# A state-space scan followed by neighbourhood attention: scan units of 64 channels and two states, with three additions handed to TensorE

## The chip, the cores and the metric

One Trainium2 chip, one of its cores. The metric is the device time of one execution in microseconds; the time before is the median of three runs. Engines are called TensorE (PE in the rows), VectorE (DVE), ScalarE (ACT), GpSimd (POOL) and SyncE (SP, which here only issues DMAs).

## The reference

Input x has 4 images of 96 channels and 1024 positions. The first layer is a bidirectional state-space model; the second, neighbourhood attention, is not touched by the change. Cut to the first:

```python
x_norm = layernorm(x_flat) * gamma + beta
x_in = jnp.concatenate([x_norm, x_norm[:, ::-1]], axis=0)      # 8 sequences of 1024 steps
xr, z = jnp.split(x_in @ W_in, 2, axis=-1)                     # 192 channels each
xr = silu(causal_depthwise_conv4(xr) + conv_b)
dbl = xr @ W_xproj                                             # 6 + 16 + 16 columns
dt = softplus(dbl[..., :6] @ W_dt + b_dt); Bm, Cm = dbl[..., 6:22], dbl[..., 22:]
def step(h, inp):                                              # 192 channels x 16 states
    h = exp(dt_t[:, :, None] * A) * h + (dt_t * x_t)[:, :, None] * B_t[:, None, :]
    return h, einsum('ben,bn->be', h, C_t)
y = (ys + xr * D) * silu(z)
out = (out_fwd + out_rev) * 0.5 + x_flat                       # out = y @ W_out
```

## The kernel before

**Tiles and units.** The 8 sequences of 192 channels are cut into 12 tiles of 128 rows (`TILE_ORDER`): an "L" tile holds channels 0 to 127 of one sequence, an "H" tile the channels 128 to 191 of two images. A tile has 16 units, one for each state, so there are 192 units k. For each unit:

- TensorE copies row n of B over all channels: two bf16 products with the 0/1 matrix `pick` (`spread_b`, L369) put it into one of two PSUM slots `bu`. The product for unit k+1 may start only when the scan of unit k-1 has freed its slot. B is held in `st` as three bf16 pieces that add up to the f32 value.
- ScalarE computes a = exp(dt * A) (`decay`, L564), two units ahead.
- VectorE multiplies `bu` by u = dt * x (`times_b`, L724) and scans along the positions (`scan`, L734).
- GpSimd multiplies the states by C (`read_out`, L690). C comes back from DRAM spread over the rows, in `c_rep`, by a DMA on SyncE's queue.
- TensorE adds the product to `y_ps` with an identity matrix (`sum_states`, L390), three units later (`SUM_LAG`).

**Work between units.** All else is a list of jobs written out by hand, `PLAN`: (unit at which TensorE starts it, name, arguments). Each job fills one of the two halves of `f_ps`, and ScalarE (VectorE for "out") empties it; a job waits until the job two before it has been emptied (`free`). In unit k TensorE issues, in this order, the B products of unit k+1, the jobs of unit k (`front`), and the sum of unit k-3. "conv" is the convolution as four taps, one tap a unit; "xp" the projection to B, C and the low-rank dt; "dt" the product before the softplus; "z" the gate; "cen" and "var" the layernorm; "out" the output product. ScalarE empties a job in the unit after its last one, behind that unit's `decay`.

**Softplus and the pieces of B.** ScalarE makes four pieces of the softplus (L505 to L519); GpSimd adds three of them (L639, L643, L647) and multiplies by x (L652). Of B, ScalarE rounds to bf16, GpSimd subtracts (L628), ScalarE rounds again (L494, L495), GpSimd subtracts again (L634). GpSimd also adds the two directions' x for the skip term D * x (L659), which VectorE adds to `y_ps` (L712) before it multiplies by the gate (L716).

**Before the first unit** the engines run the same jobs for the first tile in an order of their own (the lists in front of `for k in range(UNITS)`).

Of the kernel before, what the change touches and what calls it, by code (L numbers as in the profile page):

```python
# [9 lines left out]
ALU = mybir.AluOpType  # L10
# [11 lines left out]
A_RING, H_RING, HC_RING, C_RING, SUM_LAG = 3, 3, 4, 4, 3  # L22
ROWS = 3 * 2 * N_ST + RANK
LOADS = [4, 7, 12, 8]
# [27 lines left out]
def cols(th, n=HALF):  # L52
# [7 lines left out]
XR_SLOT = (0, 1, 2, 3, 4, 5, 3, 6, 0, 4, 1, 5)  # L60
XR_TILES = 7
STEPS = {"conv": TAPS, "xp": 2}

FIRST = [("cen", 0), ("var", 0), ("cen", 1), ("var", 1), ("conv", 0), ("conv", 2), ("xp", 0, 0), ("dt", 0),
         ("conv", 1)]

PLAN = [
# [4 lines left out]
    (49, "var", 2, 0), (50, "var", 2, 1), (51, "dt", 4, 0), (52, "dt", 4, 1), (53, "cen", 3, 0), (54, "cen", 3, 1),  # L72
    (56, "var", 3, 0), (57, "var", 3, 1), (58, "conv", 6, 0), (62, "conv", 6, 1), (66, "dt", 5, 0), (67, "dt", 5, 1),
    (68, "conv", 7, 0), (72, "conv", 7, 1), (76, "z", 1, 0), (77, "z", 1, 1), (78, "out", 0, 0, 0),
    (79, "out", 0, 0, 1), (79, "xp", 2, 0, 0), (81, "xp", 2, 0, 1), (84, "dt", 6, 0), (85, "dt", 6, 1),
    (86, "z", 2, 0), (87, "z", 2, 1), (88, "conv", 8, 0), (92, "conv", 8, 1), (97, "xp", 3, 0, 0), (99, "xp", 3, 0, 1),
    (101, "dt", 7, 0), (102, "dt", 7, 1), (103, "out", 1, 1, 0), (104, "out", 1, 1, 1), (105, "out", 2, 0, 0),
    (106, "out", 2, 0, 1), (107, "out", 2, 1, 0), (108, "out", 2, 1, 1), (109, "conv", 9, 0), (113, "dt", 8, 0),
    (114, "dt", 8, 1), (115, "conv", 9, 1), (119, "conv", 10, 0), (123, "conv", 10, 1), (128, "xp", 2, 1, 0),
# [3 lines left out]
    (168, "out", 3, 2, 0), (169, "out", 3, 2, 1), (182, "z", 5, 0), (183, "z", 5, 1), (184, "out", 4, 2, 0),  # L83
    (185, "out", 4, 2, 1), (186, "out", 4, 3, 0), (187, "out", 4, 3, 1)]
LAST = [("out", 5, 3, 0), ("out", 5, 3, 1)]
JOBS = [f + (th,) for f in FIRST for th in range(2)] + [p[1:] for p in PLAN] + LAST
# [3 lines left out]
SKIP_AT = (42, 60, 75, 142, 158, 171)  # L90
# [26 lines left out]

def mamba(nc, t, x1, bn_stats, c_d):

    with ExitStack() as ctx:  # L120
# [20 lines left out]
        pick = sb("pick", [ROWS - RANK, N_ST, 128], BF16)  # L141
# [8 lines left out]
        dt = sb("dt", [128, 2, L])  # L150
        u = sb("u", [128, 2, L])
        z = sb("z", [128, L])
        y = sb("y", [128, 3, L])
        dbc = sb("dbc", [ROWS, 4, L])
# [23 lines left out]
        st_rest = sem("st_rest")  # L178
        st_mid = sem("st_mid")
        st_done = sem("st_done")  # L180
        soft_act = sem("soft_act")
        soft = sem("soft")
        z_ready = sem("z_ready")
        skip_sum = sem("skip_sum")
        y_copied = sem("y_copied")
        y_skip = sem("y_skip")
# [14 lines left out]
        def bank(*job):  # L201
            return f_ps[:, J(*job) % 2, :]
# [13 lines left out]
        def _(sp):  # L216
            def both(column, name):
# [11 lines left out]
                 (pick_f, t["pick"]), (ident[:, :], t["ident"]), (a_neg[:, 0, :], t["A_log"][0:E_LO]),  # L229
                 (a_neg[0:E_HI, 1, :], t["A_log"][E_LO:E_IN]), (a_neg[E_HI:128, 1, :], t["A_log"][E_LO:E_IN])] +  # L230
# [6 lines left out]
            for group, done in zip(groups, loaded):  # L237
                for dst, src in group:
                    sp.dma_start(dst, src).then_inc(done, 16)
            for k in range(UNITS):  # L240
                tile, n = divmod(k, N_ST)
                if n == 0:
                    for b, d in tile_seqs(tile):
                        sp.wait_ge(c_stored[seq_slot(b, d)], 16 * (b // 2 + 1))
                if k >= C_RING:
                    sp.wait_ge(hc_done, k - C_RING + 1)
                kind, i, d = TILE_ORDER[tile]
                if kind == "L":
                    sp.dma_start(c_rep[:, k % C_RING, :], c_d[2 * i + d, n:n + 1, :].to_broadcast([128, L]))\
                        .then_inc(c_in[k % C_RING], 16)  # L250
                else:
                    for part in range(2):
                        sp.dma_start(c_rep[E_HI * part:E_HI * part + E_HI, k % C_RING, :],
                                     c_d[2 * (2 * i + part) + d, n:n + 1, :].to_broadcast([E_HI, L]))\
                            .then_inc(c_in[k % C_RING], 16)

        def c_loads(k):

            return sum(len(tile_seqs(i // N_ST)) for i in range(k % C_RING, k + 1, C_RING))
# [1096 lines left out]
```

## Time and profile before

| | |
|---|---|
| median of 3 runs | 1227.54 us (1224.55 to 1229.1) |
| the profiled execution, its own time | 1225.61 us |
| its span, first to last instruction | 1223.7 us |
| before the first unit | 0 to 55.0 us |
| the 192 units | 55.0 to 771.5 us |
| second layer | from about 782 us |
| busy in the stretch 55 to 772 us | VectorE 677.4, TensorE 642.6, GpSimd 595.6, ScalarE 440.3 of 717 us |
| granted TensorE clock there | 0.95 of 2.4 GHz on average |

The busy times add up, engine by engine, what ran; they don't tell what was waited for. That is read from the idle time just before an instruction and from what ended it. A wait of an engine that has slack costs nothing.

### The profile page before, as it was taken

To read this page: it belongs to the slowest core of one execution; us is meant where nothing else is said; L and a number is where in the kernel's file an instruction comes from. 1 tells how busy PE (TensorE), PEld (TensorE's weight loads), DVE (VectorE), ACT (ScalarE), POOL (GpSimd) and SP (SyncE) were. 2 spreads that over 40 slices of the span, in tenths; PEclk is the share of its full clock that TensorE was granted. 3 is DMA by queue.
4 is the path that set the end of the run, shared out by engine and by line. 5 is a ranking of instruction groups with operands and counts; after the bars stand their busy time and mean duration, and the time that the engine had idled before them with its cause. 6 is when DMAs were issued, how large, how long until landed. Compare 5 with 4: busy or idle time off the path is not lost. (4 is left out here: it accounts for less than half of the span.)

```text
span 1223.7 us, 9473 instructions
## 1 busy us (share of the span) xinstructions
PE 1078.3 (88%) x3294; PEld 369.1 (30%) x3294; DVE 964.5 (79%) x635; ACT 549.0 (45%) x574; POOL 878.0 (72%) x348
## 2 busy tenths in 40 slices
PE   7789999889988999989978878599999999996675
PEld 2233333333232333324322222223333333332221
DVE  1499999899998999999989999600296796969771
ACT  5755857796657464756573634111111020110321
POOL 0079799888878778978988966400098969789890
PEclk9879999899999989998988989879999999998787
DMA  2144355434354434453434444163849595682502
GB/s 78 71 141 151 140 157 137 156 123 153 121 157 123 153 122 138 136 173 126 170 121 138 133 144 136 25 153 76 129 102 188 84 204 83 141 133 39 107 1 73
DMA packets 106863, 150.95 MB, mean 123 GB/s; under 512 B 62818, under 2 KB 75848, under 8 KB 106816
## 3 DMA queue, kind: packets, MB, share of 16 engines
q1 hardware_dynamic: 104832, 143.65, 44.7%
q10 hardware_dynamic: 1984, 6.70, 2.0%
q8 instruction: 26, 0.43, 0.1%
q14 instruction: 21, 0.17, 0.1%
HBM read 123.27 MB, written 10.70 MB: 109 GB/s over the span
## 5 line engine op out<-in xcount | busy, mean ns | idle before, releaser
L690 POOL TENSOR_TENSOR hc<-h,c_rep 128x1024 f32<-128x1024 f32 x192 | 451.2, 2358 | 175.7 <-DVE h L734 169.5
L734 DVE TENSOR_TENSOR_SCAN h<-a,bu 128x1024 f32<-128x1024 f32 x192 | 439.0, 2286 | 20.1 <-ACT a L564 2.4
L390 PE MATMUL y_ps<-hc,ident 128*128 128x512 f32 x768 | 384.7, 625 | 2.9 <-POOL hc L690 1.7
L564 ACT ACTIVATE a<-dt,a_neg 128x1024 f32<-128x1024 f32 x192 | 218.6, 1148 | 224.5 <-DVE h L734 216.6
L724 DVE TENSOR_TENSOR bu<-bu,u 128x1024 f32<-128x1024 f32 x192 | 232.1, 1209 | 16.2 <-PE bu L369 16.2
L1147 POOL TENSOR_TENSOR prod_p<-vw,at 128x3584 f32<-128x3584 f32 x18 | 130.2, 7235 | 124.2 <-DMA vw<-v_d 120.8
L390 PEld LDWEIGHTS y_ps<-hc,ident 128*128 128x128 f32 x768 | 145.3, 197 | 213.3 <-issue 188.7
L1028 PE MATMUL sc_ps<-x,w_up 128*64 128x512 f32 x672 | 177.6, 604 | 0.0
L1028 PE MATMUL sc_ps<-x,w_low 96*64 96x512 f32 x672 | 177.3, 603 | 0.0
L369 PE MATMUL bu<-st,pick 96*64 96x512 bf16 (+1 forms) x512 | 120.2, 394 | 47.0 <-DVE h L734 41.3
L1098 ACT ACTIVATE sc<-sc_ps,rel 128x512 f32<-128x512 f32 x24 | 16.6, 690 | 248.4 <-PE sc_ps L1028 248.4
L1154 POOL TENSOR_TENSOR prod_p<-prod_p 128x1536 f32<-128x1536 f32 (+1 forms) x36 | 104.6, 2904 | 2.8
L1230 DVE TENSOR_REDUCE e_ps<-at 128x32 f32<-128x1568 f32 x6 | 17.6, 2932 | 106.4 <-DMA at<-scores_d 106.4
L369 PEld LDWEIGHTS bu<-st,pick 96*64 96x64 bf16 (+1 forms) x512 | 29.1, 104 | 194.7 <-DVE h L734 136.0
L1147 DVE TENSOR_TENSOR prod_v<-vw,e_ps 128x3584 f32<-128x3584 f32 (+1 forms) x24 | 86.8, 3616 | 0.5
L1250 DVE TENSOR_TENSOR acc_ps<-acc_ps,prod_v 128x1024 f32<-128x1024 f32 x66 | 81.3, 1232 | 2.3
L1028 PEld LDWEIGHTS sc_ps<-x,w_up 128*64 128x64 f32 x672 | 49.1, 137 | 100.6 <-issue 100.6
L1028 PEld LDWEIGHTS sc_ps<-x,w_low 96*64 96x64 f32 x672 | 49.3, 136 | 99.1 <-issue 99.1
L287 PE MATMUL f_ps<-xn,w_taps 96*128 96x512 f32 x128 | 68.6, 637 | 5.8 <-ACT t L507 2.9
L1044 PE MATMUL g_ps<-x,c_w 96*128 96x512 f32 x48 | 31.3, 811 | 26.6 <-DVE x L1222 26.6
L1120 ACT ACTIVATE up<-g_ps,c_b 128x512 f32<-128x512 f32 x24 | 16.5, 689 | 70.9 <-PE g_ps L1044 70.9
L564 ACT ACT_TABLE_LOAD x27 | 34.6, 1283 | 0.5
(124 smaller groups left out, 928.3 us busy)
## 6 DMA issues: line engine op xcount, KB each, us to landing
c_rep<-c_d SPq DMA_DIRECT2D x128, 512.0 KB, 3.6
c_rep<-c_d SPq DMA_DIRECT2D x128, 256.0 KB, 3.9
vw<-v_d SPq DMA_DIRECT2D x24, 532.0 KB, 9.6
x<-qk SPq DMA_DIRECT2D x66, 171.0 KB, 6.4
scores_d<-sc ACTq DMA_DIRECT2D x24, 196.0 KB
at<-scores_d SPq DMA_DIRECT2D x24, 196.0 KB, 4.7
x<-qk SPq DMA_DIRECT2D x22, 152.0 KB, 6.7
v_d<-v SPq DMA_DIRECT2D x4, 541.5 KB, 6.2
```

Of the source, the lines that this page charges most:

```text
L287: mm = pe.matmul(out, w_taps[:, j, 0:E_LO], xn[:, i, s:s + HALF], start=(j == 0), stop=(j == TAPS - 1))
L369: mm = pe.matmul(bu[rows, k % 2, cols(th)], pick[:, n, 0:rows.stop - rows.start], st[:, seq_slot(b, d), cols(th)], start=True, stop=True)
L390: mm = pe.matmul(y_ps[:, cols(th)], ident[:, :], hc[:, k % HC_RING, cols(th)], start=(n == 0 and d == 0), stop=(n == N_ST - 1))
L564: nc.scalar.activation(a[:, k % A_RING, :], dt[:, tile % 2, :], ACT.Exp, scale=a_neg[:, kind_of(tile), n:n + 1]).then_inc(exp_done, 1)
L690: nc.gpsimd.tensor_tensor(hc[:, k % HC_RING, :], h[:, k % H_RING, :], c_rep[:, k % C_RING, :], ALU.mult).then_inc(hc_done, 1)
L724: nc.vector.tensor_tensor(bu[:, k % 2, :], bu[:, k % 2, :], u[:, tile % 2, :], ALU.mult)\
L734: nc.vector.tensor_tensor_scan(scan_order(h[:, k % H_RING, :], d), scan_order(a[:, k % A_RING, :], d), scan_order(bu[:, k % 2, :], d), 0.0 ...
L1028: mm = pe.matmul(sc_ps[64 * i:64 * i + 64, th, :], w[:, dx, :], x4[0:rows, (2 * p + i) % X4_RING, y:y + 16, dx:dx + W], start=(dx == 0 and ...
L1044: pe.matmul(bank(n)[:, :], c1_w[:, 128 * m:128 * m + 128], x1[:, b, cols(th)], start=True, stop=True).then_inc(job_done, 1)
L1147: return engine.tensor_tensor(prod, shifted, e[:, lo:hi].unsqueeze(2).broadcast_to([128, hi - lo, HD, W]), ALU.mult)
L1154: nc.gpsimd.tensor_tensor(prod_p[:, lo[0]:lo[1]], prod_p[:, lo[0]:lo[1]], prod_p[:, hi[0]:hi[1]], ALU.add).then_inc(pp, 1)
L1250: nc.vector.tensor_tensor(acc_v, acc_v, prod_v[:, k:k + 2], ALU.add).then_inc(pv, 1)
```

## The change

A unit now holds 64 channels in two states: rows 0 to 63 the even state, rows 64 to 127 the odd one. Two units, one for each half of a tile's channels, follow each other, and `sum_states` adds both, with a 128x64 matrix `fold` that adds the two states as well. dt and u must therefore lie twice, once in each half of the rows: SyncE's queue copies them by halves. On TensorE there are three new kinds of jobs: "sum" adds the four pieces of the softplus, "rest" and "low" make the differences of B, and the skip term is a product with a diagonal matrix. Each is taken off GpSimd or VectorE. ScalarE empties both halves of `f_ps` in one instruction. A job that took several units, one tap or part in each, now does its first half in one unit and its second half in the next ("conv", "sum"), or both halves in one unit ("xp", "rest", "low", "dt").

```diff
-A_RING, H_RING, HC_RING, C_RING, SUM_LAG = 3, 3, 4, 4, 3
+A_RING, H_RING, HC_RING, C_RING, SUM_LAG = 3, 3, 4, 4, 4
-STEPS = {"conv": TAPS, "xp": 2}
+STEPS = {"conv": 2, "sum": 2}
...
-    (0, "xp", 1, 0, 0), (2, "xp", 1, 0, 1), (5, "dt", 1, 0), (6, "dt", 1, 1), (7, "conv", 3, 0), (11, "conv", 3, 1),
...
+    (0, "xp", 1, 0), (2, "rest", 1, 0), (3, "dt", 1), (5, "low", 1, 0), (7, "sum", 1), (9, "conv", 3), (12, "conv", 5),
+    (14, "dt", 2), (18, "sum", 2), (21, "xp", 0, 1), (23, "rest", 0, 1), (24, "conv", 4), (26, "low", 0, 1),
...
             for k in range(UNITS):
...
+                for part in range(2):
+                    sp.dma_start(c_rep[E_HI * part:E_HI * part + E_HI, k % C_RING, :],
+                                 c_d[2 * b + d, 2 * m + part:2 * m + part + 1, :].to_broadcast([E_HI, L]))\
                         .then_inc(c_in[k % C_RING], 16)
...
+                for t_next in range(1, N_TILES):
+                    since = k - AT[("sum", t_next)]
+                    if since == 6:
+                        left(sp, J("sum", t_next, 1))
+                        second_half(dt, t_next, dt_b)
+                    if since == 8:
+                        sp.wait_ge(u_done, t_next + 1)
+                        sp.wait_ge(dt_b, 32 * (t_next + 1))
+                        first_half(dt, t_next, dt_a)
+                        second_half(u, t_next, u_b)
+                    if since == 9:
+                        sp.wait_ge(u_b, 32 * (t_next + 1))
+                        first_half(u, t_next, u_a)
...
+            def rest_job(b, d, th):
+
+                rows = slice(0, ROWS - RANK)
+                out = bank("rest", b, d, th)[rows, :]
+                free(J("rest", b, d, th))
+                pe.wait_ge(st_high, SEQS.index((b, d)) + 1)
+                pe.matmul(out, ident[rows, rows], dbc[rows, b % 2, cols(th)], start=True, stop=False)
+                pe.matmul(out, minus_i[rows, rows], st[rows, seq_slot(b, d), cols(th)], start=False,
+                          stop=True).then_inc(job_done, 1)
...
+            def sum_job(tile, th):
+                n = J("sum", tile, th)
+                free(n)
+                pe.wait_ge(soft_act, 4 * tile + 4)
+                for i, part in enumerate((t3, t4, dt[:, tile % 2, 1, :], dt[:, tile % 2, 0, :])):
+                    mm = pe.matmul(bank("sum", tile, th), ident[:, :], part[:, cols(th)], start=(i == 0), stop=(i == 3))
                 mm.then_inc(job_done, 1)
...
                 for th in range(2):
-                    mm = pe.matmul(y_ps[:, cols(th)], ident[:, :], hc[:, k % HC_RING, cols(th)],
-                                   start=(n == 0 and d == 0), stop=(n == N_ST - 1))
-                mm.then_inc(summed, 1)
+                    for half in range(2):
+                        rows = slice(E_HI * half, E_HI * half + E_HI)
+                        mm = pe.matmul(y_ps[rows, cols(th)], fold[:, :], hc[:, (k + half) % HC_RING, cols(th)],
+                                       start=False, stop=(m == N_ST // 2 - 1))
+                mm.then_inc(summed, 2)
...
             for k in range(UNITS):
                 spread_b(k + 1)
+                if k >= SUM_LAG and k % 2 == 0:
+                    sum_states(k - SUM_LAG)
                 front(k)
-                if k >= SUM_LAG:
-                    sum_states(k - SUM_LAG)
...
             softplus(0)
-            middle(0, 0)
+            rest_left(0, 0)
+            low_left(0, 0)
             for th in range(2):
                 conv_left(1, th)
...
                 dve.wait_ge(summed, N_ST * (r + 1))
-                dve.wait_ge(skip_sum, g + 1)
-                nc.vector.scalar_tensor_tensor(out=y_ps[:, :], in0=xr_of(f), scalar=d_skip[:, kind:kind + 1],
-                                               in1=y_ps[:, :], op0=ALU.mult, op1=ALU.add).then_inc(y_skip, 1)
```

**TensorE before the first unit.** Before, from the end of "xp" (L307) and the dt product of the first tile (L317) over the conv of tile 1 (L287) to the B products of the first two units (L369):

```order
L307 MATMUL f_ps<-xr,w_x 102x512
L317 MATMUL f_ps<-dbc,w_dt 128x512 x2
L287 MATMUL f_ps<-xn,w_taps 128x512 x8
L369 MATMUL bu<-st,pick 128x512 x4
L303 MATMUL f_ps<-xr,w_x 102x512
```

Of the change, from the dt product to the same conv (dt L374, conv L326; L352 to L364 are "rest" and "low"):

```order
L374 MATMUL f_ps<-dbc,w_dt 128x512 x2
L352 MATMUL f_ps<-dbc,ident 96x512
L353 MATMUL f_ps<-st,minus_i 96x512
L352 MATMUL f_ps<-dbc,ident 96x512
L353 MATMUL f_ps<-st,minus_i 96x512
L362 MATMUL f_ps<-dbc,ident 32x512
L363 MATMUL f_ps<-st,minus_i 32x512
L364 MATMUL f_ps<-mid,minus_i 32x512
L362 MATMUL f_ps<-dbc,ident 32x512
L363 MATMUL f_ps<-st,minus_i 32x512
L364 MATMUL f_ps<-mid,minus_i 32x512
L326 MATMUL f_ps<-xn,w_taps 128x512 x8
```

"rest" and "low" now stand ahead of the conv of tile 1.

**TensorE around units 50 to 53,** where tile 3 begins. Before, units 50 and 51: "var" (L275) and "dt" (L317), `y` put back into `y_ps` (L387), the sums (L390) and the B products (L369):

```order
L369 MATMUL bu<-st,pick 128x512 x2
L275 MATMUL f_ps<-var,center 96x512
L390 MATMUL y_ps<-hc,ident 128x512 x2
L369 MATMUL bu<-st,pick 128x512 x2
L317 MATMUL f_ps<-dbc,w_dt 128x512
L387 MATMUL y_ps<-y,ident 128x512 x2
L390 MATMUL y_ps<-hc,ident 128x512 x2
```

Of the change, from the sums in unit 50 to the B products behind those of unit 52 ("sum" L383, `y` put back L459, skip term L461, sums L467, B products L440):

```order
L467 MATMUL y_ps<-hc,fold 64x512 x4
L383 MATMUL f_ps<-t,ident 128x512 x2
L383 MATMUL f_ps<-dt,ident 128x512 x2
L440 MATMUL bu<-st,pick 128x512 x2
L383 MATMUL f_ps<-t,ident 128x512 x2
L383 MATMUL f_ps<-dt,ident 128x512 x2
L440 MATMUL bu<-st,pick 128x512 x2
L459 MATMUL y_ps<-y,ident 128x512 x2
L461 MATMUL y_ps<-xr,diag_d 128x512 x2
L467 MATMUL y_ps<-hc,fold 64x512 x4
L440 MATMUL bu<-st,pick 128x512 x4
```

Four f32 products of "sum" now stand between two sets of B products, where there was one product of "var" or "dt" with two of the sums.

## Rows read from the trace of the kernel before

**Rows 1.** Page, part 1: busy us, share of the span, instructions.
```profile
PE 1078.3 (88%) x3294; PEld 369.1 (30%) x3294; DVE 964.5 (79%) x635; ACT 549.0 (45%) x574; POOL 878.0 (72%) x348
```
**Rows 2.** Timeline of one unit at 307 us: start, us, engine, line.
```profile
307.44 1.21 DVE L724 TENSOR_TENSOR bu<-bu,u 128x1024 f32<-128x1024 f32 x1
307.58 0.60 PE L369 MATMUL bu<-st,pick 96*128 96x512 bf16 x2
...
308.12 1.08 PE L291 MATMUL f_ps<-xn,w_taps 96*64 96x512 f32 x4
...
308.74 2.29 DVE L734 TENSOR_TENSOR_SCAN h<-a,bu 128x1024 f32<-128x1024 f32 x1
...
309.13 1.98 PE L390 MATMUL y_ps<-hc,ident 128*128 128x512 f32 x4
...
310.94 1.21 DVE L724 TENSOR_TENSOR bu<-bu,u 128x1024 f32<-128x1024 f32 x1
...
311.08 0.60 PE L369 MATMUL bu<-st,pick 96*128 96x512 bf16 x2
```
**Rows 3.** Waits of VectorE, 55 to 772 us: total us, times, longest.
```profile
DVE bu L724 <- PE bu L369: 16.2, 9, 3.9
DVE h L734 <- ACT a L564: 2.4, 3, 1.6
DVE x L702 <- PE f_ps L337: 2.2, 1, 2.2
DVE y_ps L712 <- PE y_ps L390: 1.9, 2, 1.7
DVE h L734 <- issue: 0.9, 2, 0.5
```
**Rows 4.** Groups by line: busy us, mean ns, idle before.
```profile
L712 DVE SCALAR_TENSOR_TENSOR y_ps<-xr,d_skip,y_ps 128x1024 f32<-128x1024 f32 x6 | 7.7, 1285 | 3.1 <-PE y_ps L390 2.9
...
L690 POOL TENSOR_TENSOR hc<-h,c_rep 128x1024 f32<-128x1024 f32 x192 | 451.2, 2358 | 175.7 <-DVE h L734 169.5 <-PE y_ps L390 6.2
```
**Rows 5.** Timeline of TensorE, 20 to 34 us, two convs.
```profile
19.69 7.11 PE L287 MATMUL f_ps<-xn,w_taps 96*128 96x512 f32 x16 [0.59 <-ACT var L432]
26.73 7.09 PE L291 MATMUL f_ps<-xn,w_taps 96*64 96x512 f32 x32
```
**Rows 6.** Timeline, a late B product, 224 to 232 us.
```profile
224.61 1.06 ACT L494 ACTIVATE st<-dbc 32x1024 bf16<-32x1024 f32 x1 [5.37 <-POOL dbc L628]
...
227.27 2.02 PE L271 MATMUL f_ps<-x,center 96*96 96x512 f32 x2 [5.04 <-ACT z L432]
...
231.75 0.60 PE L369 MATMUL bu<-st,pick 96*128 96x512 bf16 x2
...
232.38 1.23 DVE L724 TENSOR_TENSOR bu<-bu,u 128x1024 f32<-128x1024 f32 x1 [3.89 <-PE bu L369]
```
**Rows 7.** Timeline, TensorE at the full clock, 235 to 238 us.
```profile
235.19 1.88 PE L390 MATMUL y_ps<-hc,ident 128*128 128x512 f32 x4
...
236.91 0.60 PE L369 MATMUL bu<-st,pick 96*128 96x512 bf16 x2
...
237.35 1.02 PE L275 MATMUL f_ps<-var,center 96*96 96x512 f32 x2
```
**Rows 8.** Timeline before the first unit, 42 to 57 us.
```profile
42.19 8.83 PE L287 MATMUL f_ps<-xn,w_taps 96*128 96x512 f32 x16 [0.59 <-ACT t L507]
...
46.44 1.15 ACT L519 ACTIVATE u<-u,minus_one 128x1024 f32<-128x1024 f32 x1
...
47.62 1.05 ACT L494 ACTIVATE st<-dbc 32x1024 bf16<-32x1024 f32 x1
...
51.06 0.69 ACT L432 ACTIVATE xr<-f_ps,conv_b 128x512 f32<-128x512 f32 x1 [0.73 <-PE f_ps L287]
...
54.13 1.28 ACT L609 ACT_TABLE_LOAD   x1
...
56.61 2.29 DVE L734 TENSOR_TENSOR_SCAN h<-a,bu 128x1024 f32<-128x1024 f32 x1 [0.33 <-ACT a L564]
```
**Rows 9.** Windows: stretch, its us, busy of PE, PEld, DVE, ACT, POOL, then PEclk.
```profile
640.00:650.00 10.00, 6.69 (x22) 2.31 (x21) 9.73 (x7) 3.46 (x3) 10.00 (x5) 1.00 0.35 105
...
720.00:730.00 10.00, 7.06 (x11) 2.79 (x12) 9.79 (x7) 2.30 (x2) 4.71 (x2) 0.66 0.33 107
```
**Rows 10.** Timeline of ScalarE at a softplus, 378 to 386 us, and TensorE behind it.
```profile
378.41 1.04 ACT L512 ACTIVATE t<-t 128x1024 f32<-128x1024 f32 x1
...
382.80 1.15 ACT L519 ACTIVATE u<-u,minus_one 128x1024 f32<-128x1024 f32 x1
...
384.49 2.02 PE L287 MATMUL f_ps<-xn,w_taps 96*128 96x512 f32 x2 [2.29 <-ACT z L432]
```
**Rows 11.** DMA issues: KB each, median us to landing.
```profile
c_rep<-c_d SPq DMA_DIRECT2D x128, 256.0 KB, 3.9
```

More of the change, by code:

```diff
@@ L85 @@
-LAST = [("out", 5, 3, 0), ("out", 5, 3, 1)]
-JOBS = [f + (th,) for f in FIRST for th in range(2)] + [p[1:] for p in PLAN] + LAST
+    (0, "xp", 1, 0), (2, "rest", 1, 0), (3, "dt", 1), (5, "low", 1, 0), (7, "sum", 1), (9, "conv", 3), (12, "conv", 5),
+    (14, "dt", 2), (18, "sum", 2), (21, "xp", 0, 1), (23, "rest", 0, 1), (24, "conv", 4), (26, "low", 0, 1),
+    (28, "z", 0), (30, "dt", 3), (32, "cen", 2), (34, "sum", 3), (36, "var", 2), (38, "xp", 1, 1), (40, "rest", 1, 1),
+    (42, "low", 1, 1), (44, "cen", 3), (46, "dt", 4), (48, "var", 3), (50, "sum", 4), (54, "conv", 6),
@@ L87 @@
+    (125, "rest", 3, 1), (126, "dt", 9), (128, "low", 3, 1), (130, "sum", 9), (142, "dt", 10), (146, "sum", 10),
+    (158, "dt", 11), (162, "sum", 11), (168, "z", 4), (169, "out", 3, 2), (184, "z", 5), (186, "out", 4, 2),
+    (187, "out", 4, 3)]
+LAST = [("out", 5, 3)]
+JOBS = [j + (th,) for j in FIRST + [p[1:] for p in PLAN] + LAST for th in range(2)]
+AT = {p[1:]: p[0] for p in PLAN}
 DONE_AT = {p[1:]: p[0] + STEPS.get(p[1], 1) for p in PLAN}
@@ L240, in _, with first_half @@
+            def first_half(pairs, tile, done):
+                sp.dma_start(pairs[high, tile % 2, 0, :], pairs[low, tile % 2, 0, :]).then_inc(done, 16)
+            sp.wait_ge(soft_first, 3)
+            first_halves(dt, dt_a, dt_b, dt[:, 1, 0, :])
+            sp.wait_ge(u_done, 1)
+            first_halves(u, u_a, u_b, u[:, 1, 0, :])
             for k in range(UNITS):
[L241 to L244, printed above, removed]
+                tile, m, half, (b, d) = unit(k)
+                if k % N_ST == 0:
+                    for seq in tile_seqs(tile):
+                        sp.wait_ge(c_stored[seq_slot(*seq)], 16 * (seq[0] // 2 + 1))
@@ L257, in c_loads @@
         def c_loads(k):
-            return sum(len(tile_seqs(i // N_ST)) for i in range(k % C_RING, k + 1, C_RING))
+            return 2 * (k // C_RING + 1)
         @block.tensor
@@ new lines, in low_job @@
+            def low_job(b, d, th):
+                rows = slice(0, 2 * N_ST)
+                out = bank("low", b, d, th)[rows, :]
+                free(J("low", b, d, th))
+                left(pe, J("rest", b, d, 1))
+                pe.matmul(out, ident[rows, rows], dbc[rows, b % 2, cols(th)], start=True, stop=False)
+                pe.matmul(out, minus_i[rows, rows], st[rows, seq_slot(b, d), cols(th)], start=False, stop=False)
+                pe.matmul(out, minus_i[rows, rows], mid[rows, cols(th)], start=False,
+                          stop=True).then_inc(job_done, 1)
@@ L741, in front @@
                     if name == "out" and at == k:
[L742 to L743 removed]
+                        for th in range(2):
+                            add_out(*job, th)
+                tile, n = divmod(k - SUM_LAG + 2, N_ST)
                 if n == 0 and 0 < tile <= N_TILES and TILE_ORDER[tile - 1][2] == 1:
@@ L780, in _ @@
             for _, *job in LAST:
-                add_out(*job)
+                for th in range(2):
+                    add_out(*job, th)
             left(dve, len(JOBS))
```

453 lines of the change are left out of this document (225 added, 228 removed), and 6 rows, old and new, of the table PLAN.

## The prediction

> **What bounds the kernel now.** The page's busy times [rows 1] give TensorE the largest share of the span, but the two layers have different limits, so I read the stretches first: the change touches only the first layer, and its 192 units take 716.5 of 1223.7 us. The timeline of one unit [rows 2] shows who sets the pace there. VectorE multiplies (1.21 us), scans (2.29 us), and multiplies again 3.50 us after the first time, with no idle time between. TensorE's B product for a unit starts when the scan has freed its slot, then comes a job, then the sum, which ends at about the time when the next B product may start. VectorE is full, and TensorE nearly. 192 x 3.50 is 672 us; the rest is gates, output additions and waits. The waits of VectorE [rows 3] add up to 23.6 us, 16.2 of them for a B product. What makes one late stands in [rows 6]: ScalarE waited 5.37 us for a subtraction on GpSimd, so it emptied a bank late, TensorE waited 5.04 us for that bank, and the next B product, in line behind it, was 3.89 us late for VectorE. So of everything on the other engines only what delays a B product counts, and VectorE's own work.
>
> **What the change takes from VectorE.** The six skip additions of 1.285 us [rows 4], one of them at the very end: -7.7 us. Multiplications and scans stay 192 of each, with the same shape; a unit of 64 channels and two states is as long as one of 128 channels. GpSimd loses some five operations of about 2.4 us a tile. It was no bound (it waited 169.5 us for the scan, [rows 4]), so this gives nothing by itself, but the waits of ScalarE on it, as in [rows 6], go. I take all 23.6 us of old waits away and count the new ones afresh.
>
> **TensorE, unit by unit.** Costs at the full clock. Two f32 products of 512 columns, 1.72 us from start to start, so 0.86 each; the two B products, 0.44, taken as 0.45 [rows 7]. Products 64 columns wide, two at a time on the two halves of the array, cost 7.09 us for 8 pairs in a conv, against 7.11 us for 8 whole products [rows 5]: a pair costs as much as one. The four products with `fold` thus take 1.72 us for two units, where two units took 3.44 before. I add 0.15 for the turn from 128 to 64 columns: in [rows 2] one such pair took 1.01 us from 308.12 to the next start at 309.13, not 0.86. (TensorEngine Tiling (Array Packing) of the Trainium skill, section Key Properties, says that changing the tiling mode drains the engine; that speaks against this change, which turns twice in each two units, and the 1.01 us agrees with it.)
>
> A unit without a job thus costs TensorE 0.45 us when odd and 2.32 when even. But the new list puts half a "conv" or half a "sum", four f32 products or 3.44 us, into one unit: 3.89 us odd, 5.76 even. The start of a backward tile costs 5.76 too, without a job (0.45, 1.72 to put `y` back, 1.72 skip term, 1.87 sums). The average falls: over all units my costs sum to about 545 us, and TensorE was busy 642.6 of 717 us before. What counts is the lump. There are two slots for B: the product of unit k+1 can't start before scan k-1 ends and must be there 3.50 us later, and from its start to VectorE's go [rows 6] 0.63 us pass (231.75 to 232.38). So TensorE may be 2.87 us late and no more. I carry the lateness along (late + cost - 3.50, not below zero) and book what is over 2.87 as a wait of VectorE.
>
> - Units 50 to 52, "sum" then a backward tile's start: 2.26, 2.65, 4.91, a wait of 2.0 us. The same stands at 36, 68, 148 and 164 (at 36 with "var" in place of the put-back): five times, 10.3 us.
> - Unit 84, half a "sum" with a tile's start: 9.20 us, a wait of 4.3. Unit 116, "sum", start and "rest": 2.6.
> - Units 7 to 14, "sum", two convs, "dt": 2.8. Units 18 to 26, "sum", start, "xp", conv, "low": 3.0. Units 58 and 120, convs: 1.3 and 1.4. Units 100 and 132: 0.7 together.
>
> That is 26.4 us. By the same sums the old list, with one tap a unit, comes to no wait at all: a unit there costs 0.45 + 1.72 + 0.86, about 3.0 of 3.50 us.
>
> **ScalarE.** A softplus holds it from the first exponential to the end of the fourth piece for 5.5 us (378.41 to 383.95, [rows 10]), behind a `decay` of 1.15 and before a table load of 1.28: 8 us in a unit of 3.50. "sum" stands two units (7.0 us) behind the softplus's unit and needs all four pieces, which are ready after 6.7 us if ScalarE began on time. Where it has emptied a conv, "low" or "var" just before, it hasn't: at six tiles I find TensorE waiting for about 1 us, at unit 7 2.7, and at unit 82 ("rest" behind "xp" and softplus) 3.2. Such a wait was seen before: 2.29 us, [rows 10]. Part of it falls on lumps already late. I add 10 us (bounds 0 and, if every one of them came straight on VectorE, 14, with more where the clock is low, below).
>
> **Before the first unit.** Before, softplus ended at 47.6 us and the conv of tile 1 had begun on TensorE at 42.19 [rows 8]; ScalarE emptied its second half at 51.06, and VectorE scanned 5.5 us later, at 56.6. Now "rest" and "low" stand ahead of this conv. ScalarE now waits for both halves of "xp" and of "dt" and empties them in one go, about 0.45 us later each time, and is at 48.5 with the softplus; then two pieces of B, 1.05 us each as in [rows 8]: 50.6. "low" on TensorE, four f32 products and four bf16 ones, about 2.7: 53.3. ScalarE empties it: 54.4. The conv's first half waits for that bank, and its 8 products take 7.1 [rows 5] to 8.8 us [rows 8]: 61.5 to 63.2. From there two more table loads, the SiLU and `decay`: 5.5 us, so the first scan at 67 to 69, 10.4 to 12.1 us later than before. The row nearest in time is the 8.8, so I take +12. The copies of dt and u don't set this: u is ready at about 53.5, and four such transfers, at 3.9 us to landing for one [rows 11], are there by about 60.
>
> **SyncE's copies later.** A tile's copies are issued 6 to 9 units after "sum", and "sum" is at least 13 units ahead of its tile, except tile 1, with 9. There the last one leaves about 2.5 units ahead (C for unit k goes out when unit k-4 is read), waits for one landing, and lands again after 3.9 us; 1 to 2 us are to spare. I count nothing; without that margin it would cost up to 4 us, once.
>
> **The clock.** Full-clock costs are a lower bound. In 720 to 730 us TensorE was busy 7.06 of 10 us at a granted clock of 0.66, in 640 to 650 us with 6.69 at 1.00 [rows 9]: at that load it falls at times. Two units without a job now keep TensorE busy for 2.8 of 7.0 us, less than either row. Between jobs late in the list (units 133 to 141, 149 to 157, 170 to 183) the clock may be at 1.2 GHz when "dt", "sum" or a tile's start comes. I take 6 us for this, between 0 and 25, what the same sums give with every TensorE cost 10% up.
>
> **The sum.** -23.6 -7.7 +26.4 +10 +6 +12 = +23 us. Against the profiled execution's 1225.6 us: 1248.7. That execution was 1.9 us below the median, so **1250 us**.
>
> **Rivals.** *The lumps are hidden* (0.14, faster): TensorE's load per unit falls by a sixth, and if a lump of two units' length reached VectorE nowhere, only -23.6 -7.7 +12 stayed: 1208 us. It decides at lateness 2.87 us; against it stands that a B product 3.9 us late cost VectorE just that [rows 6]. *They cancel* (0.10): waits of 10 to 25 us where I count 42, with a shorter setup: 1222 to 1234, no change. *The clock falls* (0.12): half the clock in the sparse stretches makes half a "sum" 6.9 us long; some 10 jobs at 2 us or more: about 1270. TensorE: Matmul & The Clock Gate of the Trainium skill, Part 1, states that the throttled clock is the default and activity lifts it; by that rule this rival is likelier than I have it, and rows 9 bear it out only half. *The pairs don't overlap* (0.04): 96 x 1.72 us more, TensorE at 710 us over VectorE's 672: above 1300; [rows 5] speak against it. *Copies come late or C behind them* (0.04): some 4 us a tile, about 1290. What is left, 0.56, is the forecast, 1235 to 1262.
>
> Measurement tells about 0.5%, 6 us, from no change. Faster: the first rival and the lower tail, 0.16. Same 0.10. Slower 0.74. The range reaches from the upper part of the first rival, 1214, to the clock rival's, 1274.
>
> **What would show it.** In the profile after: first scan at 66 to 70 us; waits of VectorE on B products at 35 to 45 us in some 20 places instead of 9, the longest near the unit-84 lump; TensorE less busy in the scan stretch but VectorE with more idle time; units without lumps still at 3.50 us; no wait on u or dt copies. Wrong if VectorE's waits stay under 20 us, if the unit is no longer 3.50 us, or if the first scan starts before 62 us.

## The result, and the profile after

The changed kernel takes 1293.09 us (median of 4, 1292.78 to 1295.26) against 1226.07 (4 runs, 1224.55 to 1229.1): 1.0547 times as long, 95% interval 1.0521 to 1.0574. The forecast had the direction and was 43 us short: 1250, at most 1274. Page of the changed kernel, busy us with share and instructions, and the rows of TensorE's busy share and clock in 40 slices:

```profile
span 1290.9 us, 10118 instructions
...
PE 1101.0 (85%) x3502; PEld 342.5 (27%) x3502; DVE 959.0 (74%) x631; ACT 554.6 (43%) x542; POOL 760.4 (59%) x295
...
PE   7789898888988888899686766859999999998475
...
PEclk9659898888998888898787877769999999999777
```

VectorE lost 5.5 us of work (the six additions, less a little set-up) and GpSimd 118 [rows 1]. The granted clock fell from 0.940 of full speed to 0.881 over the span. In the scan stretch (72 to 839 us) TensorE was busy 652.6 us at a clock of 0.86; the kernel before had 641.6 us at 0.95 from 56 to 772 us. The forecast had worked out about 545 us at the full clock and expected TensorE to be less busy there. The waits of VectorE, in the stretch that answers to [rows 3]:

```profile
DVE bu L773 <- PE bu L440: 77.3, 44, 14.2
DVE x L754 <- PE f_ps L402: 9.6, 9, 2.6
DVE h L783 <- ACT a L655: 4.0, 2, 3.8
DVE bu L773 <- DMA u<-u: 1.3, 1, 1.3
DVE y L763 <- PE y_ps L467: 0.6, 1, 0.6
DVE h L783 <- issue: 0.5, 1, 0.5
```

The longest wait on a B product, 14.2, and the 3.8 for a decay stand ahead of the first scan. That leaves 63.1 us in 43 places for B, where some 20 places were expected, and 75.3 us of waits in all inside the units. (A little more is lost than these rows name: all of VectorE's idle time between the first and the last scan grew from 21.9 to 78.9 us.) Units without a lump are still 3.50 us apart, and the longest wait, 5.8 us, stands at unit 85, as the forecast said. The set-up, in the changed kernel's timeline:

```profile
43.90 1.99 PE L352 MATMUL f_ps<-dbc,ident 96*96 96x512 f32 x2 [2.26 <-ACT t L592]
...
50.67 1.88 PE L362 MATMUL f_ps<-dbc,ident 32*32 32x512 f32 x2 [2.22 <-ACT mid L571]
...
55.34 0.63 PE L364 MATMUL f_ps<-mid,minus_i 32*32 32x512 bf16 x1
...
57.13 10.01 PE L326 MATMUL f_ps<-xn,w_taps 96*128 96x512 f32 x16 [1.16 <-ACT st L516]
...
72.73 2.29 DVE L783 TENSOR_TENSOR_SCAN h<-a,bu 128x1024 f32<-128x1024 f32 x1 [3.81 <-ACT a L655]
```

The first scan starts at 72.73 us, before at 56.61 [rows 8]: 16.1 us later. From there to the end of the last scan it is 766.3 us instead of 714.9. These two, 67.5 us, are the whole change of the span (67.2). The clock of the first units, in windows (stretch, its us, busy us of PE, PEld, DVE, ACT, POOL, then PEclk, DMA share, GB/s):

```profile
40.00:50.00 10.00, 6.20 (x10) 1.74 (x8) 1.92 (x2) 8.77 (x9) 0.00 (x0) 0.62 0.04 7
50.00:60.00 10.00, 8.16 (x12) 2.43 (x13) 3.43 (x6) 1.54 (x2) 0.00 (x0) 0.50 0.71 164
60.00:70.00 10.00, 8.01 (x18) 3.10 (x16) 1.23 (x1) 3.48 (x4) 0.00 (x0) 0.84 1.04 231
70.00:80.00 10.00, 9.62 (x12) 2.09 (x12) 6.44 (x4) 7.15 (x8) 3.75 (x2) 0.50 0.22 59
80.00:90.00 10.00, 7.84 (x12) 2.83 (x12) 9.70 (x6) 6.08 (x6) 5.65 (x3) 0.50 0.53 132
```

At 0.50, 1.2 GHz, a product takes about twice as long: in the first "xp" inside the units an f32 product takes 1.93 to 1.96 us from start to start (a row with "x2" is one such product), against 0.86 at the full clock [rows 7]. That "xp", and a "sum" at unit 84:

```profile
70.38 2.00 PE L341 MATMUL f_ps<-xr,w_x 128*102 128x512 f32 x2 [2.37 <-ACT xr L552]
72.31 2.03 PE L343 MATMUL f_ps<-xr,w_x 64*102 64x512 f32 x2
74.27 2.03 PE L341 MATMUL f_ps<-xr,w_x 128*102 128x512 f32 x2
76.23 2.03 PE L343 MATMUL f_ps<-xr,w_x 64*102 64x512 f32 x2
78.19 1.89 PE L440 MATMUL bu<-st,pick 96*128 96x512 bf16 x4
...
405.17 3.78 PE L383 MATMUL f_ps<-t,ident 128*128 128x512 f32 x4 [2.68 <-ACT mid L571]
408.75 3.06 PE L383 MATMUL f_ps<-dt,ident 128*128 128x512 f32 x4
411.64 0.60 PE L440 MATMUL bu<-st,pick 96*128 96x512 bf16 x2
```

"xp" holds the line for 7.8 us from 70.38, and its unit's products of B come after it. At 405 TensorE had waited 2.68 us for ScalarE, and the four products of the first half of the "sum" took from 405.17 to about 411.6, where the forecast had 3.44 us. The lumps of units 83 to 86 cost VectorE 10.2 us, where the forecast had 4.3.

### The profile page after: what moved, and what is told of

Read it like the earlier page. It is cut to its first block and busy times, and to the rows that moved or that the text cites. A ratio compares the mean times of both kernels' runs of the same rounds, so it can differ in the third digit from the quotient of the medians.

```text
span 1290.9 us, 10118 instructions
## 1 busy us (share of the span) xinstructions
PE 1101.0 (85%) x3502; PEld 342.5 (27%) x3502; DVE 959.0 (74%) x631; ACT 554.6 (43%) x542; POOL 760.4 (59%) x295
## 5 line engine op out<-in xcount | busy, mean ns | idle before, releaser
L467 PE MATMUL y_ps<-hc,fold 128*64 128x512 f32 x768 | 238.1, 752 | 2.6 <-POOL hc L742 2.6
L440 PE MATMUL bu<-st,pick 96*128 96x512 bf16 x384 | 126.4, 424 | 98.4 <-DVE h L783 98.2
L467 PEld LDWEIGHTS y_ps<-hc,fold 128*64 128x64 f32 x768 | 55.8, 162 | 134.5 <-issue 125.6
L440 PEld LDWEIGHTS bu<-st,pick 96*128 96x128 bf16 x384 | 28.7, 100 | 228.5 <-DVE h L783 133.1
L326 PE MATMUL f_ps<-xn,w_taps 96*128 96x512 f32 x128 | 64.5, 654 | 3.2 <-ACT st L516 1.8
L383 PE MATMUL f_ps<-t,ident 128*128 128x512 f32 x88 | 44.4, 628 | 5.8 <-ACT mid L571 2.7
```

Source lines behind the costliest of these rows:

```text
L326: mm = pe.matmul(out, w_taps[:, j, 0:E_LO], xn[:, i, s:s + HALF], start=(j == 0), stop=(j == TAPS - 1))
L440: mm = pe.matmul(bu[:, k % 2, cols(th)], pick[:, 2 * m:2 * m + 2, :].rearrange("p n c -> p (n c)"), st[:, seq_slot(*seq), cols(th)], start ...
L467: mm = pe.matmul(y_ps[rows, cols(th)], fold[:, :], hc[:, (k + half) % HC_RING, cols(th)], start=False, stop=(m == N_ST // 2 - 1))
```

## The experiments

Each time is a median, beside the kernel before on the same chip (1225.3 to 1227.3 us); in brackets stands the ratio to it with its 95% interval.

**A staircase from the kernel before to the changed one.** Each kernel adds to the one before it. First the scan unit and the skip term alone:

```
-                nc.vector.tensor_tensor(bu[:, k % 2, :], bu[:, k % 2, :], u[:, tile % 2, :], ALU.mult)
+                nc.vector.tensor_tensor(bu[:, k % 2, :], bu[:, k % 2, :], u[:, tile % 2, n % 2, :], ALU.mult)
...
+                sp.dma_start(pairs[dst, tile % 2, 1, :], pairs[high, tile % 2, 0, :]).then_inc(done, 16)
```

> The kernel before with the new scan unit alone (64 channels by two states, dt and u copied by halves, sums of pairs) and the skip term on TensorE; the convolution stays at one tap per unit, the softplus additions on GpSimd and the split of B on VectorE. By the theory that lateness of TensorE (its lumps) makes the waits, TensorE has no lump over one unit's slack left, VectorE's waits on B products fall to at most 20 us in the units, and the time is about 1222 us (1212 to 1232). By the rival, that the new unit's lighter TensorE work lets the granted clock fall (to about 0.8) and half-clock products make the waits, the waits stay at 40 us or more and the time is 1240 us or more.

1283.1 us (1.0452, 1.0426 to 1.0478), clock 0.847. Neither account fits whole: the waits on B are 20.6 us, about as by the lumps' account, the clock and the time as by the rival's, and a third wait, one for the copies that neither had, holds the most:

```profile
DVE bu L764 <- DMA u<-u: 36.5, 7, 8.8
DVE bu L764 <- PE bu L407: 20.6, 13, 3.6
DVE x L745 <- PE f_ps L378: 19.7, 9, 3.2
```

So the jobs ahead of the copies were moved forward:

```
-    (0, "xp", 1, 0, 0), (2, "xp", 1, 0, 1), (4, "dt", 1, 0), (5, "dt", 1, 1),
+    (0, "xp", 1, 0, 0), (1, "xp", 1, 0, 1), (3, "dt", 1, 0), (4, "dt", 1, 1),
...
-    (135, "conv", 11, 0), (139, "conv", 11, 1), (144, "xp", 3, 1, 0), (146, "xp", 3, 1, 1), (149, "dt", 10, 0),
+    (132, "conv", 11, 0), (136, "conv", 11, 1), (140, "xp", 3, 1, 0), (141, "xp", 3, 1, 1), (144, "dt", 10, 0),
```

> The run on the layout alone had VectorE wait 36.5 us for copied halves of u, because softplus on GpSimd ended one to three units too late for the two copies behind it; that is no part of the change, which makes u earlier. Here the rank expansions of tiles 1, 6, 7, 9 and 10 and the split ahead of them are issued one to five units earlier, nothing else. By the account that those waits add to the rest, they fall below 10 us and the time is 1247 to 1258 us; the granted clock stays near 0.85. If the copies come late because the transfers themselves are slow, the waits on u stay above 20 us and the time above 1268 us.

1243.9 us (1.0132, 1.0094 to 1.017), just under what was expected. Its four runs lie between 1239.1 and 1250.6 us, and the profiled one is the slowest. The copies' wait is 8.8 us now:

```profile
DVE x L745 <- PE f_ps L378: 18.6, 9, 3.2
DVE bu L764 <- PE bu L407: 17.2, 12, 2.3
...
DVE bu L764 <- DMA u<-u: 8.8, 3, 6.9
```

Next the changed kernel's order of jobs on it, half a conv a unit and both halves of the others in one (`STEPS` 1):

```
+                    if name == "conv" and at == k:
+                        for j in range(TAPS):
+                            conv_job(*job, j)
```

> The changed kernel's own order of jobs (both halves in one unit, a half convolution a unit) on the layout kernel, with the softplus additions and the split of B left on GpSimd and VectorE, so that no job of theirs is in TensorE's line. If the unspread list makes the loss that is left and prices add up, it takes 1258 to 1268 us (about what the early layout kernel with lumped convolutions took) and the rest up to 1293 us belongs to the sums, the split of B and the set-up. If those parts on TensorE cost no more than the sums' 10.5 us and the set-up's 8.6, it takes 1272 to 1278 us.

1248.7 us (1.0174, 1.0151 to 1.0198), less than either account had. By the medians the order of jobs costs 4.8 us, but the two intervals overlap, so it may be next to nothing. In this kernel, which has no split on TensorE, the first scan starts at 64.65 us, 8.0 later than before, and what VectorE waits for ahead of it is a copied half of u:

```profile
DVE bu L766 <- DMA u<-u: 7.7, 1, 7.7
```

The forecast had the copies landed by about 60 us. Then the split of B onto TensorE, with the sums of softplus left on GpSimd. The edit is shown against the changed kernel; against the kernel of the step before, this one has more than the split: ScalarE empties both halves of a job in one instruction, `dbc` has two slots instead of four, and the copies of dt and u are issued at other units.

```
-    (5, "low", 1, 0), (7, "sum", 1), (9, "conv", 3), (12, "conv", 5),
+    (5, "low", 1, 0), (9, "conv", 3), (12, "conv", 5),
...
+                            nc.gpsimd.tensor_tensor(t4[:, :], t4[:, :], t3[:, :], ALU.add).then_inc(soft, 1)
```

> The changed kernel with one part undone: the three softplus additions are back on GpSimd, and the sum jobs leave TensorE's list; all other jobs stay at their units. Lump theory: the running sum of TensorE's costs, with ScalarE's late banks, falls from 36 to 5 us at the full clock and from 62 to 16 with every cost up by a tenth, so 30 to 46 us gained, 1247 to 1263 us, and the waits of VectorE on B products go at units 9 to 12, 36 to 38, 52 to 54, 84 to 86, 148 to 150. Clock theory alone (TensorE too idle): with 76 us less work on TensorE the clock falls further and less than 15 us are gained.

1282.6 us (1.045, 1.0434 to 1.0465), far above what the lumps' account had, and within the clock's: the clock fell to 0.848 and 10.5 us were gained. Read from below, the split of B with what came along costs 33.9 us, the largest step; read from above, the sums of softplus, which the forecast had as its main lump, cost 10.5. That is what is left of more: unit by unit, putting them on TensorE makes some units 31.1 us longer in all, above all 9 to 11, 84 and 85, and others 20.7 us shorter, among them unit 15, where u is copied sooner and the wait for it falls from 5.3 to 1.3 us. VectorE's waits on B in the kernel before this step:

```profile
DVE bu L766 <- PE bu L409: 35.4, 25, 3.3
```

And in the one with the split of B on TensorE:

```profile
DVE bu L787 <- PE bu L442: 62.6, 32, 13.1
```

The first scan starts at 64.65 us without the split on TensorE and at 73.86 with it, 9.2 us later; from the first scan to the last it is 756.0 us against 734.8, 21.2 more. (These are the profiled executions, which lie 30.9 us apart, the medians 33.9.)

**One part alone on the kernel before.** The skip term:

```
+                        mm = pe.matmul(y_ps[:, cols(th)], diag_d[:, kind_of(tile), :], xr_of(tile)[:, cols(th)],
+                                       start=(d == 0), stop=False)
```

> The kernel before with the skip term alone moved: two products of a diagonal matrix with the tile's channels at each tile's first state on TensorE (24 products of 512 columns in all, 128 wide), in place of six additions on GpSimd and six on VectorE; the scan unit, the order of jobs and the set-up stay. The six additions were 7.7 us with their wait; TensorE gains some 1.9 us of work at each of the six forward tiles and of the six reverse tiles, where it has slack. By the sum in the prediction it is 5 to 8 us faster, 1218 to 1222 us. By a rival in which TensorE's put-back of y and the skip products make the first sum of a reverse tile late, it is within 3 us of before.

1214.3 us (0.9909, 0.9894 to 0.9924), 12.4 less: faster than both kernels, and more than the 8 expected. The 7.7 us of the additions are their work alone, without the wait in front of them [rows 4]. Beside them, the waits on B fell from 16.2 to 14.0 us and those on `y` from 2.9 to 1.3, while those for a decay rose from 2.4 to 4.1. The convolutions in lumps:

```
-                    if name == "conv" and at <= k < at + TAPS:
-                        conv_job(*job, k - at)
+                        if k == (at + TAPS if joined else at if th else at + TAPS - 1):
+                            for j in range(TAPS):
+                                conv_job(tile, th, j)
```

> The kernel before with one change: the products of a convolution are issued at once (all eight of a tile where its halves stand four units apart, else the four of a half) in place of one tap per unit. By the theory of lumps it is 16 to 30 us slower than before (six places at 2.7 us, and the late silu and gate banks behind them on ScalarE), with the granted clock as before. By the rival that a full clock takes lumps in its slack, and that the waits of the changed kernel come from its lower clock, it is within 5 us of the kernel before.

1247.5 us (1.0169, 1.0151 to 1.0187) at a clock of 0.949, 20.8 more and inside the 16 to 30 expected. So lumps reach VectorE at about the price that the running sum gives, at a high clock:

```profile
DVE bu L728 <- PE bu L373: 35.2, 13, 5.1
```

**The clock by itself.** Less work for TensorE, the rest as it was:

```
+                light = n % 2 == 1 and n < N_ST - 1
+                for th in range(1 if light else 2):
+                    at = slice(0, 32) if light else cols(th)
```

> The kernel before, with the sums of y left out in seven of sixteen states (one product of 32 columns stands in their place and carries the semaphore), so that y lacks those states; about 100 us less work on TensorE, and every other engine's work, every lump and every dependency as before. If the granted clock costs nothing but what TensorE's own work takes, it is as fast as before or a few us faster (1215 to 1228). If lighter work lets the clock fall and jobs at 1.2 GHz then come late, the clock is 0.88 or less and the time is 1232 us or more although there is less to do.

1241.8 us (1.012, 1.0085 to 1.0155) at a clock of 0.863: less to do, and 15 us slower. Its runs scatter, from 1234.8 to 1246.5 us, all of them above the kernel before. The light kernel's page:

```profile
PE 1029.2 (83%) x3126; PEld 357.2 (29%) x3126; DVE 965.8 (78%) x635; ACT 547.5 (44%) x574; POOL 877.9 (71%) x348
...
PEclk8868987879887888997787877769999999999787
```

Its waits of VectorE, to be read against [rows 3]:

```profile
DVE bu L726 <- PE bu L369: 26.6, 17, 3.7
...
DVE y_ps L714 <- PE y_ps L392: 7.7, 5, 2.3
```

The control puts products of zeros in the place of what was left out:

```
+                        pe.matmul(y_ps[:, cols(th)], zero[:, :], hc[:, k % HC_RING, cols(th)], start=False, stop=False)
```

> A control of the light kernel (sums of y left out in seven of sixteen states, 1241.8 us at a clock of 0.863): the same sums are left out of y, but two products of the same size with a matrix of zeros stand in their place. If the loss came from the clock, it goes: granted clock 0.93 or more and 1224 to 1231 us. If it came from what was left out otherwise (order, semaphores), it stays at 1238 us or more.

1226.5 us (1.0006, 0.9992 to 1.0019), clock 0.937, VectorE's waits on B back at 15.2 us. With the same dependencies and order, work for nothing gave 15 us back. The light edit on the lumped kernel:

> The same edit on the kernel before with its convolutions in lumps (which took 1247.5 us at a granted clock of 0.949). If only TensorE's own work makes it late, lighter units between the lumps let it catch up sooner and it takes 1247 us or less. If the clock is what a lump's price hangs on, the clock falls below 0.90, the same lumps cost 10 us or more on top and it takes 1257 us or more.

1261.2 us (1.0272, 1.0251 to 1.0292), clock 0.860. The clock costs 13.7 us here and 15 without lumps; the lumps 19.4 us here and 20.8 at the high clock. The two add, as closely as the scatter of the light kernel lets one tell.

**Both on the new scan unit.** The lumps on the early layout kernel, with the same edit as before:

> The early layout kernel with its convolutions issued in lumps, the edit that cost 20.8 us in the kernel before at a clock of 0.949. If lumps and clock add up, it costs about 21 us here too: 1261 to 1268 us. If a lower clock makes each lump dearer (products twice as long, the slack the same), it costs 30 us or more: 1274 us or more.

1260.0 us (1.0275, 1.0253 to 1.0297), 16 more than the spread one, at a clock of 0.858: here too the low clock makes the lumps no dearer, if anything cheaper than the 21. And filling products in every second unit, on the layout kernel and on its early form:

```
+                        pe.matmul(y_ps[rows, cols(th)], zero[:, :], xn[:, 0, PAD + th * HALF:PAD + (th + 1) * HALF],
+                                  start=False, stop=False)
```

> The kernel of the run on the layout alone, with four products by a matrix of zeros (64 columns each) ahead of the B products in every second unit, which add nothing to the result; TensorE's work per unit is then about that of the kernel before. If the clock makes the waits, the granted clock rises to 0.93 or more and the time falls by 10 us or more below the run on the layout alone. If late products by their number make them, the time is the same or up to 10 us more.

> The early layout kernel (the new scan unit and the skip term on TensorE, everything else spread as before; 1243.9 us at a clock of 0.851) with four zero-matrix products of 64 columns in every second unit. If its loss against the kernel before is mostly the clock, the granted clock is 0.92 or more and it takes 1226 to 1234 us. If the loss is the copies and the order, it stays at 1240 us or more.

1272.4 us (1.0365, 1.0345 to 1.0385), 10.8 less at a clock of 0.919; and 1240.0 (1.0116, 1.0087 to 1.0145), 3.9 less at 0.926, which is within the scatter. The first gained the time that was expected, with a clock just short of 0.93; the second reached its clock and not its time. The filling has to be done as well. The waits on B even grew from 17.2 to 20.8 us in the second, while those on output products fell from 18.6 to 9.4.

**On the changed kernel.** The same filling in units without a job:

> The changed kernel with extra work on TensorE: in odd units without a job, in it or in the unit before, four products with a zero matrix go into y_ps, so that such a unit costs TensorE as much as an even one. The output is the same. Clock theory (TensorE's granted clock of 0.86 in the scan stretch, against 0.95 before, comes from its sparse units and makes the lumps longer): the clock rises to 0.92 or more, VectorE's waits on B products fall, 10 to 20 us gained, 1275 to 1283 us. Lump theory alone (the clock is not what made the waits larger than the 42 us forecast): no gain, up to 5 us lost where filling delays a B product.

1295.0 us (1.0563, 1.0543 to 1.0583): the clock rose to 0.910 and VectorE's waits on B in the units and ahead stayed at 75.7 us. At units 9 to 11 and 85 the periods are as long as without it (4.9, 4.9, 5.9; 9.4 us), so those are lumps whatever the clock; unit 84 fell from 8.1 to 6.7 us and unit 169 from 7.3 to 4.7, while unit 129 rose from 5.0 to 7.6, as it also does in the run with products of zeros in the set-up alone, further below. There was no gain, as by the lump account; but the clock stayed under the 0.92 of the other account, which so wasn't put to its full test. The set-up's order, with the conv of tile 1 ahead of the split of B:

```
+            for th in range(2):
+                conv_job(1, th)
             pe.wait_ge(set_up, 5)
             for th in range(2):
                 rest_job(0, 0, th)
```

> The changed kernel with one move ahead of the first unit: the conv of tile 1 stands before rest and low on TensorE and ScalarE, and the first two decays before the emptying of low. Theory (order of the setup): in the changed kernel the conv ran from 57.1 to 67.1 us and the first scan began at 72.7; now the conv can run from 43, and low, done at about 61, sets the start: first scan at 64 to 66 us, 7 to 8 us less in all, 1285 us. Rival (the clock sets the setup, whatever stands first): the conv alone shortens, rest and low run as late as before, first scan not before 70 us, under 3 us gained. The units after it should take the same time by both.

1289.4 us (1.0507, 1.0491 to 1.0522), first scan at 69.5: half of what was expected. That conv too ran in part at 1.2 GHz and took 9.72 us, and "low" behind it ran so throughout: 5.3 us at a clock of 0.50, ending at 65.8 where 61 was expected. So the clock was raised instead:

```
+            warm(3)
             for th in range(2):
                 rest_job(0, 0, th)
+            warm(3)
```

> The changed kernel (1293.1 us), with eight products of 512 columns by a matrix of zeros added before its first unit, where TensorE waits for ScalarE: three ahead of the first part of the split of B, three ahead of its second part, two ahead of the convolution of tile 1. If the low clock of 40 to 98 us is what makes the set-up and the first six units late, the granted clock there rises, the convolution falls from 10.0 to 7.1 to 8 us, the products of the first split (7.9 us in the changed kernel) to about 4, and it takes 1281 to 1289 us. If ScalarE's order sets the start whatever TensorE's clock, the filling products only stand in the way and it takes 1292 us or more.

1288.8 us (1.0517, 1.0483 to 1.0551). TensorE's rows:

```profile
57.73 7.03 PE L327 MATMUL f_ps<-xn,w_taps 96*128 96x512 f32 x16
...
67.99 1.54 PE L342 MATMUL f_ps<-xr,w_x 128*102 128x512 f32 x2 [2.38 <-ACT xr L561]
69.46 2.03 PE L344 MATMUL f_ps<-xr,w_x 64*102 64x512 f32 x2
```

The conv takes 7.03 us, not 10.01, "rest" and "low" 2.3 and 2.8 us, not 4.6 and 5.3 (the 7.9 expected for "rest" in the changed kernel is not what its trace has), and the first scan starts at 70.3, 2.4 us earlier; the whole is 4.3 us faster, with intervals that still overlap. The filling did more than these 2.4 us: in this execution the very first conv, ahead of all that was changed on TensorE, took 9.37 us at a clock of 0.80, against 7.11 at 1.00 in the changed kernel's, and everything behind it began 2.4 us later. From the dt product to the first scan it is 28.2 us, not 33.0. But once TensorE had waited 2.4 us for the channels it was back at 1.2 GHz, and "xp" in the first unit still took over 7 us. Last, the copies:

> The changed kernel with each copy of dt and u by halves made twice inside the units, the extra one into a spare tile, ahead of the real one on the same queue: 66 more transfers of 256 KB. Theory (the copies are hidden, one wait of 1.3 us on u was all): at most 6 us more, from tile 1 and the rows of C behind the copies, 1293 to 1299 us. Rival (copies and the bytes they move are part of the loss): what the first 17 MB cost is paid again, 15 us or more.

1300.0 us (1.0594, 1.0565 to 1.0623), 7 more by the medians, with intervals that overlap: about the most that the first account allows, and well short of the rival's 15. Twice the transfers hurt at tile 1 above all (unit 15 went from 4.9 to 8.9 us), where the margin was thin.

## Why the prediction was right in direction and wrong in size

*VectorE sets the pace, and what counts is lateness of a B product beyond 2.87 us:* right as far as it goes. Units without a lump take 3.50 us, and the lumps alone cost the kernel before 21 us. But a late output product and, at the start, a late copy count too.

*-7.7 for the skip term:* right as a term, too small as a part: alone it gave 12.4; the waits that went with the additions explain some 3 us of the rest.

*Pairs of 64 columns cost as much as one product:* right. At the full clock the four products with `fold` took 1.86 us from start to start (415.61 to 417.47), where 1.87 was worked out. *No wait on copies:* right within 1.3 us for the changed kernel, where the split is later still; without the split the copies set the first scan (64.65 us, after a wait of 7.7).

*+12 for the set-up:* it was 16.1. ScalarE had the second pieces of B ready at 50.5 us, as worked out; what was too short are TensorE's terms. "low" took 5.3 us where 2.7 was worked out (the forecast's words have four f32 products in it, the kernel has two, and 2.7 fits two), and the conv 10.0 where 8.8 was taken. With TensorE kept at the high clock by products of zeros they took 2.8 and 7.0.

*+26.4 and +10 and +6, 42 us of new waits:* this is the step that failed. The runs showed 75.3 us. At the places where the forecast had a lump, VectorE's idle time in the trace adds up to some 46 us, against 26.4 for the lumps, or 42 with what was added for ScalarE and the clock; another 28 stand where it had none, such as units 1, 4 and 5, 65, 81, 89, 93, 107 and 108, 169 and 181. Four things were too small or missing in it.

- **The clock, 6 us.** In the kernel before, taking TensorE's load down costs 14 to 15 us by itself (the light kernels and the control), with nothing else changed. The prediction had this as a rival, with a chance of 0.12 and 1270 us. The Trainium skill, TensorE: Matmul & The Clock Gate, Part 1, says that the throttled clock is the default and that activity lifts it; the trace agrees, with 0.50 from 50 to 60 us and from 70 to 90 us of the changed kernel, after stretches in which TensorE waited 1 to 2.4 us at a time for ScalarE, and it doesn't show why the clock stayed at 0.50 from 70 to 80 us, where TensorE was busy 9.62 of 10 us. The 14 to 15 us are 8 to 9 more than was booked, of 33 that were missing; whether it is as much in the changed kernel no run shows.
- **The scan unit itself.** The forecast had no wait of VectorE for it beyond the clock's. With the skip term it is 18.6 us slower than the kernel before, where the skip term alone is 12.4 faster: the first scan starts at 63.1 us instead of 56.6, and VectorE waits 18.6 us for output products and 8.8 for copies.
- **The split of B.** The forecast booked "rest", "low" and "xp" only where they stood beside another job, at their full-clock cost. As a step of the staircase, with the joint emptying by ScalarE that came along, this part costs 33.9 us, some 9 of them before the first scan. In units 1 to 5 of the changed kernel, for which the forecast had no wait at all, VectorE waited 6.0 us: period 4.36 us for unit 1, 6.02 and 6.47 for units 4 and 5, from scan to scan. There "xp", "rest" and "dt" ran at half clock.
- **The output products.** VectorE waited 9.6 us for them in nine places, before 2.2 in one [rows 3]. The forecast did not count a wait on this second line of TensorE's results.

As parts that can be left out, the lumps are worth less than the forecast had: the sums of softplus 10.5 us net, and the order of jobs at most some 5 (half a conv a unit is a far smaller lump than a whole one at 16 to 21 us). In their places they were dearer, 10.2 us against 4.3 at unit 84. The steps of the staircase are +18.6 for the scan unit with the skip term (with the skip term's own -12.4 in it, so some 31 for the unit and its copies, if the two add), +4.8, +33.9, +10.5. They sum to the whole loss by construction, so that is no check on them; and each price holds for its place in this order only.

The forecast's own sum with the measured terms, -23.6 -7.7 +75.3 +16.1, gives +60 us against 67.0. Most of what is left is idle time of VectorE that its rows of waits don't name.

Open: how the 21 us or so of that step inside the units divide between the split's work on TensorE, the joint emptying by ScalarE, the moved copies and the clock. No run separates them: a filling raises the clock and takes time itself, and neither the split nor the joint emptying was tried alone on the kernel before.

## What to carry to other kernels

Where an engine's products are on time only because it runs at its full clock, taking work off it can make the kernel slower: find the granted clock in the stretches that you are about to lighten, and price the jobs after them at 1.2 GHz too (here "low" took 5.3 us instead of 2.7, half a "sum" 6.5 instead of 3.44). Take the parts of a change singly; here one of them (the skip term, -12.4 us) was worth having, and the rest hid it. Let each step of such a staircase change one thing; the largest one here changed several and can't be read further. And keep jobs spread over the units: the same convolutions issued at once cost 16 to 21 us.

## What the runs showed of the hardware that was not expected

With 84 of 192 units lightened, the mean granted clock over the span fell from 0.940 to 0.863, and TensorE's busy time only from 1078.3 to 1029.2 us: part of the work saved came back as slower products. A price for lumps (19.4 to 20.8 us) and one for the clock (13.7 to 15) added up instead of multiplying, though a product takes about twice as long at 1.2 GHz. Eight products of zeros put ahead of a conv made it 3 us shorter (10.01 to 7.03 us). And the same first conv of a kernel, with the same jobs before it on TensorE, took 7.11 us in one execution and 9.37 in another, by the clock that it met, and all behind it moved by 2.4 us: so small a shift of the first scan need not come from the edit.
